# Layer 1 attention of a two-layer transformer: key and query transposes behind the scores of their slot, their evictions behind the block transpose and the block write

## The chip, the cores and the metric

The kernel runs on one NeuronCore of a Trainium2 chip, in one launch. The metric is the device time of the whole program in microseconds. A core has five engines that run their own instruction streams and meet only at semaphores: TensorE (PE in the profile; its weight loads are PEld), VectorE (DVE), ScalarE (ACT), GpSimd (POOL) and SyncE (SP), which here only issues DMA transfers. ScalarE issues one kind of transfer too; an engine that issues a transfer does so in its own program order. Each engine executes in order, so a wait holds everything behind it on that engine.

## The reference, cut to what matters

Two transformer layers on 1024 tokens of width 512, all in float32, with a layer norm after each part: a linear attention, a mixture of low-rank experts, a softmax attention and a quantised MLP. The change is in the softmax attention of layer 1:

```python
q = rmsnorm((hidden_states @ Wq + bq).reshape(b, n, H, HD), gq)     # H = 32, HD = 128
k = rmsnorm((hidden_states @ Wk + bk).reshape(b, n, H, HD), gk)
v = (hidden_states @ Wv + bv).reshape(b, n, H, HD)
scores = jnp.einsum('bhnd,bhmd->bhnm', q, k) * HD ** -0.5
out = jnp.einsum('bhnm,bmhd->bnhd', softmax(scores), v).reshape(b, n, H * HD)
return out @ Wo + bo
```

Scores are 1024 x 1024 for each head.

## The kernel before, in words

Float32 products are made of three matmuls (`three_pass`, L82 to L84): each operand is split into a high part, which ScalarE copies, and a low part, the rest, which VectorE or GpSimd subtracts. A value that comes from TensorE is therefore evicted from PSUM twice, high by ScalarE and then low by VectorE, which waits for the high part.

Layer 1's attention (`l1_attention`) is written out by hand as one stream for each engine. The outer loop goes over heads; one turn is called a step here, step h for head h. A step has eight slots, s = 0 to 7, one for each tile of 128 tokens. In slot s of step h these pieces of several heads stand side by side:

- TensorE: in even slots half of the value product of an earlier tile pair (`values`), then the projection of one tile of the next head to keys, queries and values (`project_tile`, 12 matmuls), in odd slots the transposes of a pair of tiles of keys and queries of head h + 1 (`transpose_kq`, four transposes, L1423), then `scores(h, b, s)` (six matmuls), `output_tile`, and in odd slots half of the value product.
- ScalarE, in this order: in even slots the squares for the norm; in odd slots the high part of values (`v_high`); in even slots the high part of an output pair; in odd slots the high parts of keys and queries (`kq_high`, L1325 and L1326); in even slots the high part of the transposed probabilities of a pair of tiles (`prob_hi`, L1354, two copies) and the scaling of keys and queries by their inverse norm (`scale_kq`, L1345); then `write_blocks(h, s - 1)`, a transfer issued from ScalarE (L1359); then `exponent(h, b, s)` (L1365); last, weight copies: for attention weights (`split_high`, L1039) in slots 1, 2 and 4, for the output weights in slot 3.
- VectorE: in even slots the mean squares (`means`); the projected tile plus bias (`take`, L1491); an output pair's low part or the inverse sums (in turn); in odd slots `kq_low` (L1507 and L1508); then `transpose_blocks(h, s - 1)` (L1521), then `maxima(h, b, s)` (L1515), the row maximum that `exponent` needs; then `add_output`.
- GpSimd: the inverse norms (`inverse_rms`), the low parts of values, of the probabilities (`prob_lo`, L1287) and of the weights.

The probabilities of a tile are transposed through memory: VectorE transposes within 32 x 32 blocks (L1521), ScalarE writes the tile to a buffer in HBM (512 KB, L1359), and SyncE reads it back block-wise with four transfers of 128 KB (`move`, L1242) into the place where `prob_hi` takes it. `move` waits for the landed write of its tile and, for each pair, for a free buffer. Tile 7 of head h is transposed, written and read back in slot 0 of step h + 1, and `prob_hi` takes tiles 6 and 7 in slot 2 of that step. SyncE's program for a step begins with the load of the attention weights of head h + 2 (768 KB, L1033) and of its bias (192 KB, L1227); they stand behind `move(h - 1, 6)` of the step before and ahead of `move(h - 1, 7)`:

```python
def step(h, b, cur, rest, nxt, more):
    if cur and more:
        aw.load(sp, w, h + 2)
        load_bias(h + 2, b)
    if rest:
        move(h - 1, NT - 1)
    for t in range(NT - 1):
        if cur:
            move(h, t)
```

`more` is false in steps 30 and 31, so these have no load and no weight copies. `cur` says that the head of this step has scores, `rest` that there is a head before, `nxt` that there is one after. Steps -2 to 1 and 30 to 32 are written out, the others are turns of a loop of two steps. The score sums have two buffers (`s_ps`), the tiles of keys and queries being transposed one (`kq_ps`), of which `transpose_kq` waits to be free by `kq_lo_done`.

Of the kernel before, what the change touches and what calls it, by code (L numbers as in the profile page):

```python
# [74 lines left out]
def f(ap):  # L75

    return ap.bitcast(F32)
# [972 lines left out]
def l1_attention(nc, sh, ln_in, ln, aw, mlp, w, ow, bias, bo, gains):  # L1050
# [16 lines left out]
    with ExitStack() as ctx:  # L1067
# [108 lines left out]
        def projected(h, b, nxt, more, s):  # L1176

            if s < 6:
                return (h + 1, 1 - b, s + 2) if nxt else None
            return (h + 2, b, s - 6) if more else None  # L1180
# [129 lines left out]
        @block.scalar  # L1310
        def _(act):
            for t in range(NT):
                ln_in.scalar_high(act, ln_banks, t)

            def square(g, i):
                act.wait_ge(taken, NT * g + BATCH * (i + 1))
                wait(act, summed, NB * g + i)
                act.activation(sq[:, :, :, :].rearrange("p t k d -> p t (k d)"), nat[i][:, :, 0:2 * HD],
                               ACT.Square).then_inc(squared, 1)

            def kq_high(g, bg, i):
                cut = slice(i * WIDE, (i + 1) * WIDE)
                act.wait_ge(kq_tr, NB * g + i + 1)
                wait(act, scored, NT * (g - 1))
                act.activation(k_hi[bg][:, cut], kq_ps[:, 0, :], ACT.Copy)  # L1325
                act.activation(q_hi[bg][:, cut], kq_ps[:, 1, :], ACT.Copy, scale=gain[:, 0:1]).then_inc(kq_hi_done, 1)  # L1326

            def v_high(g, bg, i):
                act.wait_ge(taken, NT * g + BATCH * (i + 1))
                wait(act, pv, NB * (g - 1))  # L1330
                act.activation(v_hi[bg][:, BATCH * i:BATCH * (i + 1), :], nat[i][:, :, 2 * HD:],
                               ACT.Copy).then_inc(v_hi_done, 1)

            def out_hi(h, i):
                act.wait_ge(pv, NB * h + i + 1)
                wait(act, y_done, NT * h + BATCH * (i - 1))
                act.activation(by_tile(o_hi[i % 2]), by_group(o_ps), ACT.Copy).then_inc(o_hi_done, 1)

            def scale_kq(g, bg, i):

                act.wait_ge(rstd_ready, NB * g + i + 1)
                for u in range(BATCH):
                    for k in range(2):
                        part = nat[i][:, u, k * HD:(k + 1) * HD]
                        last = act.activation(part, part, ACT.Copy, scale=rstd[bg][:, BATCH * i + u, k:k + 1])  # L1345
                last.then_inc(kq_scaled, 1)

            def prob_hi(h, i, part):

                act.wait_ge(moved[i % 2], MOVED * (2 * h + i // 2 + 1))  # L1350
                wait(act, pv, NB * h + i - 1)
                cut = slice(part * NT // 2, (part + 1) * NT // 2)
                raw, hi = (half[:, :, :, cut, :].rearrange("p g u m q -> p (g u) (m q)") for half in (pT_lo[i % 2], pT_hi[i % 2]))
                act.activation(hi, f(raw), ACT.Copy).then_inc(pT_hi_done, 1)  # L1354

            def write_blocks(h, t):

                act.wait_ge(blocked, NT * h + t + 1)
                act.dma_start(bounce[t % BOUNCES][:, :, :, :].rearrange("g p a n -> (g p) (a n)"),  # L1359
                              blocks[t % 2][:, :, :, :].rearrange("p a m q -> p (a m q)")).then_inc(written[t % 2], 16)  # L1360

            def exponent(h, b, t):
                act.wait_ge(shift_done, NT * h + t + 1)
                wait(act, blocked, NT * h + t - 1)
                act.activation(prob[t % 2][:, :], s_ps[t % 2][:, :], ACT.Exp, bias=shift[:, t:t + 1],  # L1365
                               accum_out=row_sum[:, t:t + 1]).then_inc(exp_done, 1)

            def step(h, b, cur, rest, nxt, more):
                if peeled(h, -1):
                    act.wait_ge(gain_ready, 1)  # L1370
                for s in range(NT):
                    if nxt and s % 2 == 0:
                        square(h + 1, s // 2)
                    if v_batch(h, b, cur, nxt, s):
                        v_high(*v_batch(h, b, cur, nxt, s))
                    q = quarter(h, b, cur, rest, s)
                    if q and q[3]:
                        out_hi(q[0], q[2])
                    if nxt and s % 2:
                        kq_high(h + 1, 1 - b, s // 2)  # L1380
                    if split_batch(h, cur, rest, s):
                        for part in range(2):
                            prob_hi(*split_batch(h, cur, rest, s), part)
                    if nxt and s % 2 == 0:
                        scale_kq(h + 1, 1 - b, s // 2)
                    if rest and s == 0:
                        write_blocks(h - 1, NT - 1)
                    if cur and s:
                        write_blocks(h, s - 1)
                    if cur:  # L1390
                        exponent(h, b, s)
                    if cur and s == 3:
                        act.wait_ge(ow_in, 16 * (h + 1))
                        wait(act, y_done, NT * (h - 1))
                        act.activation(ow_hi[b][:, :], ow_raw[:, :], ACT.Copy).then_inc(ow_hi_done, 1)
                    if nxt and more and s in SPLITS:
                        aw.split_high(act, h + 2, b, SPLITS[s])

            steps(act, step)

        @block.tensor
        def _(pe):
# [58 lines left out]
            def step(h, b, cur, rest, nxt, more):  # L1461
                for s in range(NT):
                    if s % 2 == 0 and quarter(h, b, cur, rest, s):
                        values(*quarter(h, b, cur, rest, s))
                    if projected(h, b, nxt, more, s):
                        project_tile(*projected(h, b, nxt, more, s))
                    if nxt and s % 2:
                        transpose_kq(h + 1, s // 2)
                    for t in scored_in(h, cur, s):
                        scores(h, b, t)  # L1470
                    if output(h, b, cur, rest, s):
                        output_tile(*output(h, b, cur, rest, s))
                    if s % 2 and quarter(h, b, cur, rest, s):
                        values(*quarter(h, b, cur, rest, s))
# [4 lines left out]
        def _(dve):  # L1479
# [65 lines left out]
            def step(h, b, cur, rest, nxt, more):  # L1545
                if peeled(h, -1):
                    dve.wait_ge(const_in, 32)
                    ln.link(dve, dve.tensor_tensor(gain[:, :], gain_in[:, 0:1], gain_in[:, 1:2], ALU.mult))
                    dve.tensor_scalar(gain[:, :], gain[:, :], float(HD) ** -0.5, None,
                                      ALU.mult).then_inc(gain_ready, 1)  # L1550
                    dve.wait_ge(gain_ready, 1)
                for s in range(NT):
                    q = quarter(h, b, cur, rest, s)
                    if nxt and s % 2 == 0:
                        means(h + 1, s // 2)
                    if projected(h, b, nxt, more, s):
                        take(*projected(h, b, nxt, more, s))
                    if peeled(h, -1):

                        dve.wait_ge(ln_in.tr, s + 1)  # L1560
                        dve.tensor_tensor(sh.x_nat[:, s, :], sh.x_nat[:, s, :], bo_sb[:, :], ALU.add).then_inc(
                            bias_added, 1)
                    if q and not q[3]:
                        invert_sums(q[0], q[2])
                    if q and q[3]:
                        out_lo(q[0], q[2])
                    if nxt and s % 2:
                        kq_low(h + 1, 1 - b, s // 2)

                    if rest and s == 0:  # L1570
                        transpose_blocks(h - 1, NT - 1)
                    if cur and s:
                        transpose_blocks(h, s - 1)
                    for t in scored_in(h, cur, s):
                        maxima(h, b, t)
                    if output(h, b, cur, rest, s):
                        add_output(*output(h, b, cur, rest, s))
# [350 lines left out]
```

## Time and profile before

| | |
|---|---|
| Median of 3 runs | 3117.12 us (3116.02 to 3117.77) |
| Profiled execution, its own time | 3121.27 us |
| Its span, first to last instruction | 3119.4 us |
| Mean granted clock of TensorE | 0.985 of full speed |
| TensorE busy | 2969.7 us, 95% of the span |
| VectorE busy | 1933.6 us, 62% |
| ScalarE busy | 1474.9 us, 47% |
| GpSimd busy | 1574.7 us, 50% |

Layer 1's attention reaches from about 1242 to 2856 us of the span, its scores from 1281.7 to 2820. A row of the timeline is one instruction, or several alike merged: its start and duration in us, engine, line, what it writes and reads, how many, and in brackets how long the engine sat idle before it and what ended that. Starts of TensorE's matmuls are closer together than their durations, since they are pipelined. ACTq and SPq are issues of transfers; their duration is that of the issue, not of the transfer.

### The profile page before, as it was taken

Reading aid. Unit: us, or ns where it says so; the run is one execution under the profiler, and the core shown is the slowest. Engines: PE = TensorE matmul, PEld = TensorE weight load, DVE = VectorE, ACT = ScalarE, POOL = GpSimd, SP = SyncE. Lnnn points to the kernel's source line nnn. Section 1 sums busy time; section 2 is a strip of 40 time slices with the busy share of each in tenths; the row PEclk is TensorE's granted clock in tenths of the full one; section 3 lists DMA queues with packets and bytes.
Section 4 is the critical chain, followed back from the end, with each engine's and each line's share of the span. In section 5 each row is a group of like instructions: output and inputs, shape, how many; then the busy total and the mean of one; then the engine's idle time right before and its main releaser. Section 6 shows DMA issues by size and latency. Waiting matters only on the chain. (4 is left out here: it accounts for less than half of the span.)

```text
span 3119.4 us, 56941 instructions
## 1 busy us (share of the span) xinstructions
PE 2969.7 (95%) x17632; PEld 2675.7 (86%) x17632; DVE 1933.6 (62%) x3061; ACT 1474.9 (47%) x2887; POOL 1574.7 (50%) x1075
## 2 busy tenths in 40 slices
PE   7999999999999978899999999999999999996998
PEld 7999999999999966799888898898988889885886
DVE  3445454545445455677777777777777777775565
ACT  3333333333333322566666666666666666653221
POOL 3333333333333331366666666666666666654764
PEclk9999999999999989999999999999999999998999
DMA  4112111122112101366665666666666566665551
GB/s 127 59 51 61 56 59 50 54 62 61 50 54 60 49 24 39 104 206 201 195 203 187 201 202 196 204 194 198 199 194 203 191 200 200 195 197 180 152 140 49
DMA packets 311499, 413.83 MB, mean 133 GB/s; under 512 B 35968, under 2 KB 242832, under 8 KB 311312
## 3 DMA queue, kind: packets, MB, share of 16 engines
q1 hardware_dynamic: 273728, 278.05, 31.7%
q10 hardware_dynamic: 37680, 135.02, 10.9%
q8 instruction: 32, 0.52, 0.1%
q14 instruction: 27, 0.22, 0.0%
q0 software_dynamic: 32, 0.02, 0.0%
HBM read 259.85 MB, written 136.31 MB: 127 GB/s over the span
## 5 line engine op out<-in xcount | busy, mean ns | idle before, releaser
L1365 ACT ACTIVATE b_prob<-b_s_ps,b_shift 128x1024 f32<-128x1024 f32 x256 | 285.4, 1115 | 479.1 <-DVE b_shift L1515 471.9
L82 PE MATMUL b_pj_kq<-b_w_hi,xT_hi 128*128 128x384 f32 x1008 | 344.5, 342 | 7.9 <-DVE b_nat L1491 6.6
L506 ACT ACTIVATE a_sig<-a_pj 128x512 f32<-128x512 f32 x192 | 114.9, 599 | 487.4 <-PE a_pj L84 487.3
L83 PE MATMUL b_pj_kq<-b_w_lo,xT_hi 128*128 128x384 f32 x1008 | 342.5, 340 | 0.0
L84 PE MATMUL b_pj_kq<-b_w_hi,xT_lo 128*128 128x384 f32 x1008 | 342.2, 340 | 0.0
L1287 POOL TENSOR_TENSOR b_pT_lo<-b_pT_lo,b_pT_hi 128x1024 fp32r<-128x1024 f32 x128 | 303.7, 2394 | 68.4 <-ACT b_pT_hi L1354 68.4
L1521 DVE STREAM_TRANSPOSE b_blocks<-b_prob 128x1024 f32<-128x1024 f32 x256 | 316.1, 1235 | 1.7 <-ACT b_prob L1365 1.7
L1287 POOL TENSOR_TENSOR pT_lo<-pT_lo,pT_hi 128x1024 fp32r<-128x1024 f32 x128 | 304.7, 2403 | 14.9 <-ACT pT_hi L1354 14.9
L82 PE MATMUL a_pj<-b_w_hi,xT_hi 128*128 128x256 f32 x1024 | 296.0, 289 | 11.3 <-DVE xT_lo L647 11.3
L1515 DVE TENSOR_REDUCE b_shift<-b_s_ps 128x1 f32<-128x1024 f32 x256 | 303.5, 1186 | 3.0 <-PE b_s_ps L84 3.0
L401 POOL TENSOR_TENSOR b_w_lo<-b_w_raw,b_w_hi 128x512 fp32r<-128x512 f32 x96 | 123.8, 1290 | 332.2 <-ACT b_w_hi L457 325.3
L84 PE MATMUL a_pj<-b_w_hi,xT_lo 128*128 128x256 f32 x1024 | 290.3, 283 | 0.0
L83 PE MATMUL a_pj<-b_w_lo,xT_hi 128*128 128x256 f32 x1024 | 289.9, 283 | 0.0
L1272 POOL TENSOR_TENSOR b_rstd<-b_mean_sq,power 128x4 f32<-128x4 f32 x128 | 128.9, 1007 | 305.0 <-DVE b_mean_sq L1501 298.4
L706 DVE TENSOR_TENSOR a_kv_nat<-a_pj,a_sig 128x512 f32<-128x512 f32 x128 | 88.6, 692 | 274.1 <-ACT a_sig L506 272.8
L711 DVE TENSOR_TENSOR a_acc<-a_acc,a_y_ps 128x512 f32<-128x512 f32 x252 | 170.6, 677 | 136.0 <-PE a_y_ps L84 136.0
L82 PE MATMUL b_s_ps<-b_k_hi,b_q_hi 128*128 128x512 f32 x512 | 213.4, 417 | 6.3 <-ACT b_prob L1365 6.3
L82 PEld LDWEIGHTS a_pj<-b_w_hi,xT_hi 128*128 128x128 f32 x1024 | 195.0, 190 | 14.1 <-issue 11.3
L82 PEld LDWEIGHTS b_pj_kq<-b_w_hi,xT_hi 128*128 128x128 f32 x1008 | 190.5, 189 | 19.4 <-POOL b_w_lo L1046 5.1
L84 PE MATMUL b_s_ps<-b_k_hi,b_q_lo 128*128 128x512 f32 x512 | 203.6, 398 | 0.0
L83 PE MATMUL b_s_ps<-b_k_lo,b_q_hi 128*128 128x512 f32 x512 | 203.2, 397 | 0.0
L83 PEld LDWEIGHTS a_pj<-b_w_lo,xT_hi 128*128 128x128 f32 x1024 | 195.4, 191 | 2.6
(257 smaller groups left out, 8830.7 us busy)
## 6 DMA issues: line engine op xcount, KB each, us to landing
bounce<-b_blocks ACTq DMA_DIRECT2D x256, 512.0 KB, 2.7
pT_lo<-bounce SPq DMA_DIRECT2D x512, 128.0 KB, 3.1
b_pT_lo<-bounce SPq DMA_DIRECT2D x512, 128.0 KB, 2.8
b_w_raw<-in_w SPq DMA_DIRECT2D x32, 768.0 KB, 5.7
b_w_raw<-in_w SPq DMA_DIRECT2D x95, 256.0 KB, 3.2
a_k_raw<-a_k_blocks SPq DMA_DIRECT2D x512, 32.0 KB, 1.8
a_w_raw<-in_w SPq DMA_DIRECT2D x32, 256.0 KB, 2.7
a_ow_raw<-in_ow SPq DMA_DIRECT2D x32, 256.0 KB, 3.1
```

The costliest lines, as they stand in the source:

```text
L82: pe.matmul(out, w_hi, x_hi, start=first, stop=False)
L83: pe.matmul(out, w_hi, x_lo, start=False, stop=False)
L84: return pe.matmul(out, w_lo, x_hi, start=False, stop=last)
L401: pool.tensor_tensor(w_lo[t][:, :, :], w_raw[t][:, :, :], f(w_hi[t][:, :, :]), ALU.subtract).then_inc(w_lo_done, 1)
L506: act.activation(out, pj[half][:, :], ACT.Sigmoid).then_inc(sig, 1)
L706: dve.tensor_tensor(out, pj[half][:, :], sig_tmp[half][:, :], ALU.mult).then_inc(silu, 1)
L711: dve.tensor_tensor(acc[:, t, :], acc[:, t, :], y_bank(h, t)[:, :], ALU.add).then_inc(y_added, 1)
L1272: pool.tensor_tensor(rstd[bg][:, BATCH * i:BATCH * (i + 1), :].rearrange("p t k -> p (t k)"), mean_sq[:, :, :].rearrange("p t k -> p (t k) ...
L1287: pool.tensor_tensor(lo, f(lo), f(hi), ALU.subtract).then_inc(pT_lo_done, 1)
L1365: act.activation(prob[t % 2][:, :], s_ps[t % 2][:, :], ACT.Exp, bias=shift[:, t:t + 1], accum_out=row_sum[:, t:t + 1]).then_inc(exp_done, 1)
L1515: dve.tensor_reduce(shift[:, t:t + 1], s_ps[t % 2][:, :], AX_X, ALU.max, negate=True).then_inc(shift_done, 1)
L1521: dve.transpose(blocks[t % 2][:, :, :, :].rearrange("p a m q -> p m a q"), prob[t % 2][:, :].rearrange("p (m a q) -> p m a q", a=GROUPS, q ...
```

## The change

In each odd slot the pieces that belong to the transposes of keys and queries move behind others of the same slot, on three engines:

```diff
 # ScalarE
-                    if nxt and s % 2:
-                        kq_high(h + 1, 1 - b, s // 2)
                     if split_batch(h, cur, rest, s):
...
                     if cur and s:
                         write_blocks(h, s - 1)
+                    if nxt and s % 2:
+                        kq_high(h + 1, 1 - b, s // 2)
                     if cur:
                         exponent(h, b, s)
 # TensorE
+                    for t in scored_in(h, cur, s):
+                        scores(h, b, t)
                     if nxt and s % 2:
                         transpose_kq(h + 1, s // 2)
-                    for t in scored_in(h, cur, s):
-                        scores(h, b, t)
                     if output(h, b, cur, rest, s):
                         output_tile(*output(h, b, cur, rest, s))
 # VectorE
-                    if nxt and s % 2:
-                        kq_low(h + 1, 1 - b, s // 2)
-
                     if rest and s == 0:
                         transpose_blocks(h - 1, NT - 1)
                     if cur and s:
                         transpose_blocks(h, s - 1)
+                    if nxt and s % 2:
+                        kq_low(h + 1, 1 - b, s // 2)
                     for t in scored_in(h, cur, s):
                         maxima(h, b, t)
```

Even slots keep their order, and no instruction or transfer is added or taken away.

## Rows read from the trace of the kernel before

**Rows 1.** Waits of steps 1 to 29: us in total, times, longest.
```profile
PE b_pj_kq L1423 <- ACT b_nat L1345: 41.2, 29, 2.1
ACT b_pT_hi L1354 <- DMA b_pT_lo<-bounce: 70.6, 29, 3.1
DVE b_nat L1491 <- PE b_pj_kq L84: 7.0, 19, 0.7
```

**Rows 2.** TensorE's timeline, slots 3 and 5 of step 15.
```profile
2026.53 0.66 PE L1423 MATMUL b_pj_kq<-ident,b_nat 128*128 128x128 f32 x4 [1.18 <-ACT b_nat L1345]
2026.94 0.48 PE L82 MATMUL b_s_ps<-b_k_hi,b_q_hi 128*128 128x512 f32 x1
...
2028.41 0.40 PE L82 MATMUL b_y_ps<-b_ow_hi,b_o_hi 128*128 128x512 f32 x1
...
2038.27 0.60 PE L1423 MATMUL b_pj_kq<-ident,b_nat 128*128 128x128 f32 x4
```

**Rows 3.** ScalarE's timeline: exponentials of step 1, step 15 and step 30.
```profile
1337.31 1.12 ACT L1365 ACTIVATE b_prob<-b_s_ps,b_shift 128x1024 f32<-128x1024 f32 x1 [3.14 <-DVE b_shift L1515]
...
2018.66 1.12 ACT L1365 ACTIVATE b_prob<-b_s_ps,b_shift 128x1024 f32<-128x1024 f32 x1 [3.14 <-DVE b_shift L1515]
...
2026.38 1.10 ACT L1365 ACTIVATE b_prob<-b_s_ps,b_shift 128x1024 f32<-128x1024 f32 x1
...
2038.55 1.11 ACT L1365 ACTIVATE b_prob<-b_s_ps,b_shift 128x1024 f32<-128x1024 f32 x1 [0.80 <-DVE b_shift L1515]
...
2044.37 1.12 ACT L1365 ACTIVATE b_prob<-b_s_ps,b_shift 128x1024 f32<-128x1024 f32 x1 [3.15 <-DVE b_shift L1515]
...
2050.34 1.12 ACT L1365 ACTIVATE b_prob<-b_s_ps,b_shift 128x1024 f32<-128x1024 f32 x1 [0.91 <-DVE b_shift L1515]
...
2055.63 1.12 ACT L1365 ACTIVATE b_prob<-b_s_ps,b_shift 128x1024 f32<-128x1024 f32 x1 [3.14 <-DVE b_shift L1515]
...
2061.65 1.12 ACT L1365 ACTIVATE b_prob<-b_s_ps,b_shift 128x1024 f32<-128x1024 f32 x1 [0.89 <-DVE b_shift L1515]
...
2748.73 1.12 ACT L1365 ACTIVATE b_prob<-b_s_ps,b_shift 128x1024 f32<-128x1024 f32 x1 [3.14 <-DVE b_shift L1515]
...
2754.70 1.12 ACT L1365 ACTIVATE b_prob<-b_s_ps,b_shift 128x1024 f32<-128x1024 f32 x1 [0.91 <-DVE b_shift L1515]
```

**Rows 4.** Timelines of SyncE and ScalarE, step 15; last, the page's transfers (KB, landing).
```profile
2011.37 0.36 SPq L1033 DMA_DIRECT2D b_w_raw<-in_w  x1
2012.18 0.33 ACTq L1359 DMA_DIRECT2D bounce<-b_blocks  x1
2018.57 1.90 SPq L1242 DMA_DIRECT2D b_pT_lo<-bounce  x4
2023.30 1.06 ACT L1354 ACTIVATE b_pT_hi<-b_pT_lo 128x1024 fp32r<-128x1024 f32 x1 [2.12 <-DMA b_pT_lo<-bounce]
...
bounce<-b_blocks ACTq DMA_DIRECT2D x256, 512.0 KB, 2.7
```

**Rows 5.** Timelines of ScalarE and VectorE, slot 7 of step 15.
```profile
2051.75 0.37 ACT L1325 ACTIVATE b_k_hi<-b_pj_kq 128x256 fp32r<-128x256 f32 x1
2052.52 0.42 DVE L1507 TENSOR_TENSOR b_k_lo<-b_pj_kq,b_k_hi 128x256 fp32r<-128x256 f32 x1 [1.03 <-ACT b_q_hi L1326]
2053.25 1.23 DVE L1521 STREAM_TRANSPOSE b_blocks<-b_prob 128x1024 f32<-128x1024 f32 x1
2054.41 1.19 DVE L1515 TENSOR_REDUCE b_shift<-b_s_ps 128x1 f32<-128x1024 f32 x1
```

**Rows 6.** Timelines of ScalarE and VectorE in the tail, step 31.
```profile
2797.84 1.10 ACT L1365 ACTIVATE b_prob<-b_s_ps,b_shift 128x1024 f32<-128x1024 f32 x1
2799.07 1.25 DVE L1521 STREAM_TRANSPOSE b_blocks<-b_prob 128x1024 f32<-128x1024 f32 x1 [0.18 <-ACT b_prob L1365]
2800.34 0.33 ACTq L1359 DMA_DIRECT2D bounce<-b_blocks  x1
2800.77 1.12 ACT L1365 ACTIVATE b_prob<-b_s_ps,b_shift 128x1024 f32<-128x1024 f32 x1 [1.43 <-DVE b_blocks L1521]
```

## The prediction, made before the changed kernel ran

> **What bounds the kernel now.** The change touches only the attention of layer 1, so I read that stretch, in this order. First the waits of steps 1 to 29. TensorE has one kind: the key and query transposes (L1423) wait for ScalarE's scaled keys and queries (L1345), 29 times, once per step, 41.2 us in all [rows 1]. Its own pace comes from its timeline: two sets of transposes with no stall between them start 11.74 us apart, so a step of four such pairs is 46.96 us of TensorE work [rows 2].
>
> Next the exponentials (L1365), one per slot, as a clock of the softmax side. From exponential 1 of step 1 to exponential 1 of step 30 lie 2748.73 - 1337.31 = 1411.42 us, 48.67 a step [rows 3]. TensorE needs 46.96, so 1.71 a step is lost. Is it lost in TensorE's stall, or in another chain that the stall merely shows? The rows speak for the second: before nearly every exponential ScalarE sat idle until VectorE's row maximum [rows 3], and VectorE waited for TensorE's projections only 7.0 us in 29 steps [rows 1]. ScalarE and VectorE run a chain of their own: exponential, key and query evictions, block transpose, maximum, next exponential. In one step its intervals are, slot 1 to 2: 7.72 (2026.38 - 2018.66), 2 to 4: 12.17, 4 to 5: 5.82, 5 to 6: 5.97, 6 to 7: 5.29, 7 to 0: 6.02 [rows 3]. Slots 0 to 1 do the work of 6 to 7, 5.29; 2 to 3 does that of 4 to 5, with a weight copy on ScalarE that costs 5.82 - 5.29 = 0.53; so 3 to 4 is 12.17 - 5.82 = 6.35. The sum is 48.28, this step's period.
>
> The long one, 1 to 2, holds ScalarE's wait for a transfer: the high part of the probabilities (L1354) waits for the last blocks of the head before, 29 times, 70.6 us, 2.43 a step [rows 1], 2.12 in the step shown [rows 4]. ScalarE's path there is 2023.30 - 2.12 - 2018.66 = 2.52 before that wait and 2026.38 - 2023.30 = 3.08 behind it: 5.60 plus the wait. The path over VectorE I take from step 30, whose slot 2 has no wait: 2754.70 - 2748.73 = 5.97 [rows 3], plus the weight copy that step 30 lacks, 0.53, is 6.50. So of the mean 2.43, 0.90 is free and 1.53 is paid. Without that wait the chain would take 47.1 a step: two limits 0.2 apart, TensorE's and the chain's.
>
> Why is the transfer late? Block write 7 is issued at 2012.18 and its first read back at 2018.57: 6.39 us, where the median write lands in 2.7. Beside it runs the 768 KB weight load, which SyncE issued 0.81 before, at 2011.37 [rows 4]. In SyncE's program the load comes right behind the reads of tile 6, and those wait for write 6.
>
> **The change part by part.** Nothing is added or removed; three moves in each odd slot.
>
> TensorE: four transposes go behind the six score matmuls. The work is the same. The wait they meet (mean 41.2 / 29 = 1.42, longest 2.1 [rows 1]) now comes after the scores, 2028.41 - 2026.94 = 1.47 from their start to that of the output tile [rows 2], and behind it stand the output tile and half of the values, no longer the scores. For this stall alone the cover is about complete.
>
> ScalarE and VectorE: the odd interval from one exponential to the next. Before: exponential, key copy 1.41 later (2051.75 - 2050.34), VectorE's low parts 0.77 later, block transpose 0.73, maximum 1.16, exponential 1.22 (2055.63 - 2054.41): 5.29 [rows 3, 5]. After: the block transpose needs only the exponential. From the exponential to the block transpose is 1.23 and from there to the issue of the write 1.27, read in the tail, where VectorE stood idle waiting for the exponential [rows 6]. The key copy is now queued behind the issue; the tail shows ScalarE's next instruction 0.43 behind one (2800.77 - 2800.34) [rows 6]. Then 0.77, 0.73 and 1.22 as before: 1.23 + 1.27 + 0.43 + 0.77 + 0.73 + 1.22 = 5.65. Value copy and weight copy now lie beside the block transpose, in which ScalarE waits anyway, so all four odd slots cost 5.65: 22.60 against 5.29 + 5.82 + 5.82 + 5.29 = 22.22. The change makes this part 0.38 a step longer. The uncertain piece is what an issue costs the instruction behind it: nothing if the two ran side by side, and at most the 1.11 by which exponential 7 trails its issue (2055.63 - 2053.25 - 1.27), though that is the maximum's time; at 1.11 a step would be 50.2. I take 0.43, the only row where the next instruction comes right behind.
>
> The key copy also needs the transposes, now later on TensorE: scores 1.47, then the transposes 0.41 (2026.94 - 2026.53), some 2.1 behind the start of the scores with the way to ScalarE. The scores start within 0.6 us of the exponential before (2026.94 against 2026.38) [rows 2, 3], the key copy comes 1.23 + 1.27 + 0.43 = 2.93 behind it. Cost nothing; if TensorE fell over 0.2 further back, the interval would grow one for one, but TensorE would then be the late one and nothing on it would wait for this.
>
> Transfers: the writes of tiles 0, 2, 4 and 6 are issued 2.50 behind the exponential instead of 1.41 + 0.77 + 0.73 + 1.27 = 4.18, so 1.68 earlier. SyncE's queue follows: reads of tile 6, weight load, bias load. Write 7 (an even slot, order unchanged) comes 5.65 - 5.29 = 0.36 later. So the load leads write 7 by 0.81 + 1.68 + 0.36 = 2.85 instead of 0.81. From load to landed write took 7.20 (2018.57 - 2011.37). If the same bytes take the same time, write 7 lands 4.35 behind its issue, 2.04 sooner; if the load is wholly out of its way, 2.7 behind, 3.7 sooner; if contention keeps it as it is, 0. I take 2.04, the one that the rows carry. The reader in slot 2 comes 0.36 later by the longer interval 0 to 1. New wait: 2.43 - 2.04 - 0.36 = 0.03, in the worst step (3.1 [rows 1]) 0.7. Up to 0.90 is free, so the paid 1.53 is gone.
>
> Sum of a step: 22.60 + 6.50 + 6.35 + 5.97 + 6.02 = 47.44 against 48.67: 1.23 less, over 29 steps 35.7. Step 30 has no weight copies to hide and no wait in slot 2: its four odd slots give back 1.4; step 0 perhaps 0.5. Net 33.8. The profiled execution took 3121.3 us, so 3087.5; it lay 4.2 above the median of the runs, 3117.1, and in those terms the forecast is 3083.
>
> The Trainium skill (Perfetto Trace Analysis, Identifying the Most-Contended Engine) says to find the engine with the highest occupancy and optimize that one first. By that rule closing TensorE's gaps is the whole prize, the first rival below, about 3069; the exponentials' rows show a second chain just behind, so the rule would promise some 14 us too much here.
>
> **Rivals.**
> TensorE takes over: the chain comes out at or under 46.96, as it would if the key copy ran beside the issue (odd slots 5.65 - 0.43 = 5.22, a step 45.7). Then 1.71 x 29 = 49.6 is saved, less what the edges give back: 3069. For it: the stall is real. Against it: the 0.43 row.
> Part of the wait stays: write 7 lands only about 1 us sooner and the chain still pays 0.2 to 0.9 a step: 3089 to 3109.
> Hidden anyway: the landing does not move. The wait shrinks only by the 0.36 of its later reader, slots 0 to 2 together stay as they are, the other three odd slots change by +0.36 - 0.17 - 0.17: 48.7 a step, and TensorE's stall only changes place. 3117 to 3120. For it: the 41.2 us on TensorE are no bound of their own.
> Slower: the earlier writes fall into the reads of the odd tiles. Today tile 5's write is issued in slot 6, 1.16 + 1.22 - 1.27 = 1.11 before exponential 6; it lands 2.7 later, the four reads take 1.90 to issue and the last lands 2.83 on (2023.30 - 2018.57 - 1.90) [rows 4]: 6.3 behind exponential 6. Its copy in slot 0 comes 5.29 + 2.52 - 0.53 = 7.3 behind it: slack 1.0, with the longer interval 1.3. Tile 3 for slot 6 has 1.3 too (6.3 against 5.82 + 1.99, less 0.17). Write 6 would now be issued 2.50 behind exponential 6, in the flight of those reads, and write 4 likewise. If each is stretched as write 7 is today, 6.39 - 2.7 = 3.7, slots 0 and 6 pay 3.7 - 1.3 - 0.9 = 1.5 each: 3.0 - 1.23 = 1.8 x 29, with the edges 3170. It decides from a stretch of 2.8 on. Against it: 512 KB meet 512 KB there, where write 7 meets 960 KB and reads as well. The Trainium skill (DMA: Bandwidth & Descriptors, Issuing engines are not separate DMA queues) has transfers from ScalarE and SyncE interleave on the same engines, which is what makes the collision possible; the 6.39 agrees.
>
> **How the numbers follow.** Forecast 0.50 (own range 3078 to 3090), TensorE takes over 0.14, part of the wait 0.16, hidden 0.09, slower 0.11. The range holds the first three: 3064 to 3112. A difference under 0.2% (6 us) cannot be told from none. Faster 0.80, same 0.09, slower 0.11.
>
> **What would show it.** Right: L1354's wait for a transfer falls below 0.9 a step; the odd exponential intervals are all near 5.65; write 7 to its first read near 4.4; the load 1.7 earlier against exponential 6; a step 47.4. Wrong: odd intervals near 5.2 or over 6; write 7 still over 6 us; L1354 waiting in slots 0 or 6; value matmuls waiting for the low parts where the transposes waited.

## The result, and the profile after

The changed kernel takes 3101.23 us in the median (3099.54 to 3102.95, 5 runs) against 3117.12 (3114.54 to 3117.77, 5 runs): ratio 0.9948, 95% interval 0.9937 to 0.9959, 15.9 us faster. I had forecast 33.8. The sign is right and the time lies between the outer bounds that I gave, 3064 and 3112, but outside the forecast's own range, 3078 to 3090: 15.9 of the 33.8 us came.

First the waits of ScalarE and TensorE over the steps 1 to 29 of the kernel after; the same view as [rows 1].

```profile
ACT b_prob L1365 <- DVE b_shift L1515: 319.6, 224, 2.0
ACT b_k_hi L1325 <- DVE b_blocks L1521: 148.5, 117, 1.5
ACT b_pT_hi L1354 <- DMA b_pT_lo<-bounce: 11.3, 23, 1.1
...
PE b_pj_kq L82 <- DVE b_nat L1491: 12.4, 54, 0.5
```

The 70.6 us that ScalarE waited for the last blocks are 11.3. TensorE's stall of 41.2 at the transposes is gone too; what it waits for instead, 12.4 us, is VectorE taking the projected tile out of the bank. A new wait of 148.5 us stands on ScalarE: the key copy for the block transpose, the queue order that the change made.

Now the clock of the softmax side, as in [rows 3]: four of ScalarE's exponentials of the kernel after, 6 and 7 of step 15 and 0 and 1 of step 16.

```profile
2040.36 1.12 ACT L1365 ACTIVATE b_prob<-b_s_ps,b_shift 128x1024 f32<-128x1024 f32 x1 [0.92 <-DVE b_shift L1515]
2046.16 1.12 ACT L1365 ACTIVATE b_prob<-b_s_ps,b_shift 128x1024 f32<-128x1024 f32 x1 [2.01 <-DVE b_shift L1515]
2052.18 1.12 ACT L1365 ACTIVATE b_prob<-b_s_ps,b_shift 128x1024 f32<-128x1024 f32 x1 [0.88 <-DVE b_shift L1515]
2057.99 1.12 ACT L1365 ACTIVATE b_prob<-b_s_ps,b_shift 128x1024 f32<-128x1024 f32 x1 [2.02 <-DVE b_shift L1515]
```

The odd intervals, 2046.16 - 2040.36 and 2057.99 - 2052.18, are 5.80 and 5.81, the even one 6.02 as before. In nearly all steps the odd intervals are 5.80 or 5.81, and the interval 1 to 2 is 6.38 or 6.44 where it was 7.4 to 8.7. Over the 29 steps the four odd intervals make 23.21 in place of 22.19, the four even ones 24.77 in place of 26.48. From the first exponential of step 1 (1333.09) to that of step 30 (2724.30) the 29 steps take 47.97 us each in place of 48.67.

Inside an odd interval, VectorE and ScalarE of the kernel after, slot 7 of step 15; the rows that answer to [rows 5] and [rows 6].

```profile
2041.69 1.25 DVE L1521 STREAM_TRANSPOSE b_blocks<-b_prob 128x1024 f32<-128x1024 f32 x1 [0.18 <-ACT b_prob L1365]
2042.97 0.33 ACTq L1359 DMA_DIRECT2D bounce<-b_blocks  x1
2043.40 0.38 ACT L1325 ACTIVATE b_k_hi<-b_pj_kq 128x256 fp32r<-128x256 f32 x1 [1.53 <-DVE b_blocks L1521]
2044.18 0.42 DVE L1507 TENSOR_TENSOR b_k_lo<-b_pj_kq,b_k_hi 128x256 fp32r<-128x256 f32 x1 [1.25 <-ACT b_q_hi L1326]
2044.92 1.22 DVE L1515 TENSOR_REDUCE b_shift<-b_s_ps 128x1 f32<-128x1024 f32 x1
```

Exponential to block transpose 1.33, to the issue 1.28, to the key copy 0.43, to the low parts 0.78, to the maximum 0.74, to the exponential 1.24. ScalarE sits idle in the first half and VectorE in the second: the two engines take turns.

Last SyncE's and ScalarE's issues around write 7 of the kernel after, as in [rows 4].

```profile
2046.96 1.73 SPq L1242 DMA_DIRECT2D b_pT_lo<-bounce  x4
2049.20 0.36 SPq L1033 DMA_DIRECT2D b_w_raw<-in_w  x1
2050.99 0.33 ACTq L1359 DMA_DIRECT2D bounce<-b_blocks  x1
2055.94 1.77 SPq L1242 DMA_DIRECT2D b_pT_lo<-bounce  x4
```

The load now leads write 7 by 1.79 instead of 0.81, and the first read of what it wrote is issued 4.95 us after the write instead of 6.39; over the loop's steps the means are 4.92 and 6.33.

### The profile page after: what moved, and what is told of

The parts are those of the page before. It is cut to its first block and busy times, and to the rows that moved or that the text cites. A ratio compares the mean times of both kernels' runs of the same rounds, so it can differ in the third digit from the quotient of the medians.

```text
span 3097.8 us, 56941 instructions
## 1 busy us (share of the span) xinstructions
PE 2976.4 (96%) x17632; PEld 2666.8 (86%) x17632; DVE 1946.6 (63%) x3061; ACT 1490.4 (48%) x2887; POOL 1574.9 (51%) x1075
## 5 line engine op out<-in xcount | busy, mean ns | idle before, releaser
L82 PE MATMUL b_pj_kq<-b_w_hi,xT_hi 128*128 128x384 f32 x1008 | 351.7, 349 | 21.6 <-DVE b_nat L1491 20.1
L82 PE MATMUL a_pj<-b_w_hi,xT_hi 128*128 128x256 f32 x1024 | 295.6, 289 | 11.9 <-DVE xT_lo L647 11.3
L401 POOL TENSOR_TENSOR b_w_lo<-b_w_raw,b_w_hi 128x512 fp32r<-128x512 f32 x96 | 123.7, 1289 | 332.3 <-ACT b_w_hi L457 325.4
L82 PE MATMUL b_s_ps<-b_k_hi,b_q_hi 128*128 128x512 f32 x512 | 201.9, 394 | 6.5 <-ACT b_prob L1365 6.5
L1046 POOL TENSOR_TENSOR b_w_lo<-b_w_raw,b_w_hi 128x512 fp32r<-128x512 f32 x96 | 124.0, 1293 | 151.3 <-ACT b_w_hi L1039 133.6
```

Of the source, the lines that this page charges most:

```text
L82: pe.matmul(out, w_hi, x_hi, start=first, stop=False)
L401: pool.tensor_tensor(w_lo[t][:, :, :], w_raw[t][:, :, :], f(w_hi[t][:, :, :]), ALU.subtract).then_inc(w_lo_done, 1)
L1046: pool.tensor_tensor(self.lo[b][:, :, cut], self.raw[:, :, cut], f(self.hi[b][:, :, cut]), ALU.subtract).then_inc(self.lo_done, 1)
```

## The experiments

Theory A: ScalarE and VectorE's chain sets the step, and the gain is the shorter wait for the last blocks. Theory B: the gain is TensorE's, whose stall now stands behind the scores. "Before" in the ratios is the kernel before, run beside each of them. "Step" is the mean of steps 1 to 29 in each trace. ScalarE's part alone can't run: its key copy would wait for the block transpose, which on VectorE would stand behind the low parts, and these wait for the key copy.

| kernel | median us | ratio to before, 95% interval | step us |
|---|---|---|---|
| whole change | 3101.2 | 0.9948 (0.9937 to 0.9959) | 47.97 |
| TensorE's part alone | 3134.4 | 1.0056 (1.0043 to 1.0070) | 49.24 |
| VectorE's and ScalarE's parts | 3101.1 | 0.9954 (0.9940 to 0.9967) | 48.00 |
| VectorE's part alone | 3066.4 | 0.9843 (0.9829 to 0.9856) | 46.98 |
| VectorE's and TensorE's parts | 3068.2 | 0.9854 (0.9841 to 0.9868) | 46.96 |
| before, load late | 3181.2 | 1.0218 (1.0200 to 1.0236) | 50.94 |
| whole, load late | 3235.4 | 1.0386 (1.0369 to 1.0402) | 52.76 |
| before, load and copies late | 3086.6 | 0.9907 (0.9892 to 0.9922) | 47.60 |
| whole, load and copies late | 3116.5 | 1.0003 (0.9994 to 1.0012) | 48.56 |
| VectorE's part, load and copies late | 3063.4 | 0.9834 (0.9820 to 0.9847) | 46.91 |
| whole, write issued behind the copies | 3099.7 | 0.9937 (0.9924 to 0.9950) | 46.3 and 49 to 51 in turn |

**TensorE's part alone.** The diff is the TensorE part of the change.

> One part alone: only TensorE's transposes of keys and queries go behind the scores; ScalarE and VectorE keep the order of before. Theory A (the chain of ScalarE and VectorE sets the step, and the change gained by taking the wait for the last blocks out of slot 2): that wait stays at some 2.4 us a step, the step stays near 48.6 us, TensorE's stall moves elsewhere: 3114 to 3122 us, no gain. Theory B (the gain came from TensorE's stall, which now stands behind the scores): the step falls towards 46.96, at least the 16 us that the whole change gave: 3076 to 3101 us.

Measured: 17 us slower than before. Its waits in steps 1 to 29:

```profile
ACT b_pT_hi L1354 <- DMA b_pT_lo<-bounce: 68.6, 29, 2.9
...
PE b_pj_kq L82 <- DVE b_nat L1491: 24.3, 29, 0.9
PE b_pj_kq L1423 <- ACT b_nat L1345: 15.5, 27, 1.0
ACT b_k_hi L1325 <- PE b_pj_kq L1423: 14.1, 50, 0.5
```

TensorE's stall fell from 41.2 to 15.5 and the kernel got slower. Theory B is out. The wait for the last blocks stayed (68.6), and the key copy, still at its early place, now waits for the transposes: the odd intervals 6 to 7 and 0 to 1 grew from 5.30 to 5.57 and 5.77 in the mean, those with a weight copy stayed. Theory A foretold the missing gain but not this loss.

**VectorE's and ScalarE's parts**, TensorE as before.

> The other two parts: evictions of keys and queries behind block transpose and block write on VectorE and ScalarE, transposes ahead of the scores as before. Theory A: odd intervals 5.81, slot 2's wait for a transfer under 0.9, step 48.0: 3099 to 3104 us, the time of the whole change. Theory B: TensorE still meets its stall ahead of the scores, so 3115 us or more.

Measured: the time, the step and the odd intervals (5.80, 5.81) of the whole change. TensorE's part is worth nothing in it: its stall at the transposes is 2.9 us in 29 steps here though its order is untouched.

**VectorE's part alone.**

```diff
                     if q and q[3]:
                         out_lo(q[0], q[2])
-                    if nxt and s % 2:
-                        kq_low(h + 1, 1 - b, s // 2)
...
                     if cur and s:
                         transpose_blocks(h, s - 1)
+                    if nxt and s % 2:
+                        kq_low(h + 1, 1 - b, s // 2)
```

> VectorE's part alone: kq_low behind the block transpose; ScalarE copies keys and queries ahead of the block write as before, so the copies lie beside the block transpose. Theory A: odd interval = exponential to block transpose 1.33, to the low parts 1.16, 0.74, 1.24 = 4.5 (4.7 with a weight copy), writes of even tiles as early as in the whole change, chain some 44 us a step, so TensorE's 46.96 sets it: 3117 - 1.6 x 29 = 3070 us. Theory B: nothing is changed on TensorE, its stall stays: 3112 to 3120 us.

Measured: 3066.4, 51 us under before and 35 under the whole change. Slot 3 of step 15, on ScalarE and VectorE, from exponential 2 to exponential 3:

```profile
1997.58 1.12 ACT L1365 ACTIVATE b_prob<-b_s_ps,b_shift 128x1024 f32<-128x1024 f32 x1 [0.21 <-DVE b_shift L1515]
1999.14 1.23 DVE L1521 STREAM_TRANSPOSE b_blocks<-b_prob 128x1024 f32<-128x1024 f32 x1
1999.52 0.37 ACT L1325 ACTIVATE b_k_hi<-b_pj_kq 128x256 fp32r<-128x256 f32 x1
2000.29 0.42 DVE L1507 TENSOR_TENSOR b_k_lo<-b_pj_kq,b_k_hi 128x256 fp32r<-128x256 f32 x1
2002.27 1.12 ACT L1365 ACTIVATE b_prob<-b_s_ps,b_shift 128x1024 f32<-128x1024 f32 x1 [2.02 <-DVE b_shift L1515]
```

The key copy runs while VectorE transposes the blocks. The odd interval is 4.69 here, where a weight copy stands ahead of the key copy, and 4.5 in the mean where none does. With that the chain has room and the step is TensorE's. The waits of steps 1 to 29:

```profile
DVE b_nat L1491 <- PE b_pj_kq L84: 147.0, 230, 1.4
...
ACT b_pT_hi L1354 <- DMA b_pT_lo<-bounce: 51.5, 36, 2.9
...
PE b_pj_kq L1423 <- ACT b_nat L1345: 1.4, 4, 0.6
```

TensorE's stall at the transposes is 1.4 us in all, and VectorE now waits 147.0 us for TensorE's projections, where it waited 7.0. A wait for the last blocks is still there (51.5) and costs little or nothing: where it is 18.3, with load and copies late, the time is only 3 us lower.

**VectorE's and TensorE's parts.** Against the whole change only ScalarE's order differs.

> VectorE's and TensorE's parts, ScalarE as before: differs from the whole change only in that the copies of keys and queries are issued ahead of the block write. Theory A: the copies wait for the transposes, not for the block transpose and the issue of the write, TensorE sets the step at 46.96: 3068 to 3075 us. Theory B: same as the whole change, 3101 us, since TensorE's order is the same.

Measured: 3068.2, within 2 us of VectorE's part alone, with the step at TensorE's 46.96. So the 33 us between this kernel and the whole change are ScalarE's part of it, the eviction behind the block write.

**The load late.**

```diff
-                if cur and more:
-                    aw.load(sp, w, h + 2)
-                    load_bias(h + 2, b)
                 if rest:
                     move(h - 1, NT - 1)
+                if cur and more:
+                    aw.load(sp, w, h + 2)
+                    load_bias(h + 2, b)
```

> The kernel before with one edit on SyncE: the load of the attention weights and bias is issued behind the reads of tile 7 instead of ahead of them; all orders on TensorE, ScalarE and VectorE are those of before. If the load is what makes write 7 land 6.4 us late: it lands in about 2.7, slot 2's wait for a transfer falls below 0.9, odd intervals stay 5.29 and 5.82, step 47.1: 3117 - 1.4 x 29 = 3073 to 3080 us. If the load isn't the cause: wait and step stay, 3115 to 3119 us.

> The whole change with the same SyncE edit (weight load behind the reads of tile 7). Theory A says that the changed kernel pays nothing for the transfer any more and that its odd intervals of 5.81 set the step: 48.0 stays, 3099 to 3103 us, though the late load is gone. If a part of the transfer's wait is still paid in the changed kernel: the step falls by that part, down to 47 and 3075 us.

Both times missed by a long way, because the edit brought a wait that I had not counted. ScalarE's waits for transfers in the kernel before with the late load, steps 1 to 29:

```profile
ACT b_w_hi L1039 <- DMA b_w_raw<-in_w: 98.2, 29, 5.1
...
ACT b_pT_hi L1354 <- DMA b_pT_lo<-bounce: 2.9, 1, 2.9
```

The wait for the last blocks is gone (70.6 to 2.9) and write 7 is read back 2.63 us after its issue, so the load is what made it late. The load did not lose its neighbour, it changed it: write 0 of the head that follows, which the load now meets, takes 7.2 us to its first read instead of 3.4, and almost nothing waits for that one. But the weights themselves now come too late for their first copy in slot 1 (3.4 us each time), and TensorE waits behind it, 71.9 us here and 106.9 in the whole change. The pair says nothing clean on the step, hence the next.

**Load and copies late.** As above, with one line more; on the kernel before, the whole change, and VectorE's part.

```diff
-        SPLITS = {1: 0, 2: 1, 4: 2}
+        SPLITS = {2: 0, 3: 1, 4: 2}
```

> The kernel before with the weight load behind the reads of tile 7, and the three weight copies (high and low) one slot later where the load would not have landed: in slots 2, 3 and 4 instead of 1, 2 and 4. So neither the collision nor a wait for the weights is left. If the late landing of write 7 is what cost 1.5 us a step: odd intervals 5.29 to 5.82, step 47.1, 3117 - 1.5 x 29 = 3070 to 3080 us. If the chain pays something else instead: step over 48 and 3100 us or more.

> The whole change with the same two edits (weight load behind the reads of tile 7, weight copies in slots 2, 3 and 4). Theory A: the changed kernel pays nothing for the transfer; its four odd intervals of 5.81 and even ones of 24.8 set the step at 48.0, so 3099 to 3103 us again. If part of the transfer's wait were still paid: below 3095 us.

> VectorE's part alone with the same two edits. Its step stood at 47.0 with TensorE free of stalls, so theory A (TensorE's 46.96 is the floor there, not the transfer) has it unchanged: 3064 to 3068 us. If the wait for the transfer (50.6 us in all in that kernel) were paid: 3040 to 3055 us.

ScalarE's waits for the last blocks, first in the kernel before, then in the whole change, with both edits:

```profile
ACT b_pT_hi L1354 <- DMA b_pT_lo<-bounce: 1.3, 1, 1.3
```

```profile
ACT b_pT_hi L1354 <- DMA b_pT_lo<-bounce: 0.6, 1, 0.6
```

The kernel before gains 29 us and has a step of 47.60, not the 47.1 expected; the whole change loses 15 and misses its forecast too. Both for one reason: a copy moved from slot 1 to slot 3 takes 0.5 from the interval 1 to 2 (5.86 or 5.92) and adds 1.1 to 3 to 4 (7.5), 0.6 a step. With that taken off, the whole change stands at 48.56 - 0.6, its own 47.97: it pays nothing for the transfer, which is what the run was to tell. The kernel before, so corrected, stands at 47.0 against 48.67: the late landing cost it 1.7 a step, of which 1.6 in the interval 1 to 2. The correction is taken from the whole change and is not itself a run. VectorE's part alone moves by 3 us and the intervals of its two ratios overlap: it is at TensorE's floor.

**The issue behind the copies.** On the whole change:

```diff
                     if cur and s:
-                        write_blocks(h, s - 1)
+                        act.wait_ge(blocked, NT * h + s)
                     if nxt and s % 2:
                         kq_high(h + 1, 1 - b, s // 2)
+                    if cur and s:
+                        write_blocks(h, s - 1)
```

> The whole change with one edit in the odd slots of ScalarE: the copies of keys and queries still wait for the block transpose, but stand ahead of the issue of the block write instead of behind it. It measures the price of the issue by itself. In the trace of the changed kernel the copy starts 0.43 us behind the issue, so the odd interval should fall from 5.81 to 5.38 and the chain to 46.3 a step, under TensorE's 46.96: the step is then TensorE's, 3101 - 1.0 x 29 = 3072 us (3068 to 3080), though the writes of even tiles go out some 0.7 us later. If the issue costs the chain nothing and only the wait for the block transpose does: step 48.0, 3098 to 3103 us.

Measured: the odd interval is 5.38, as forecast, against 5.80 or 5.81, so the issue costs the chain 0.43, but the time hardly moved. One step in two takes 46.3, the other 49 to 51. The pauses behind the slow ones lie in slot 0, at the start of a turn of the loop, where ScalarE stops twice with nothing to wait for; first its timeline, then the instruction queue in the page of that kernel, last the same queue between 1946 and 1960 us:

```profile
1949.99 0.63 ACT L1318 ACTIVATE b_sq<-b_nat 128x512 f32<-128x512 f32 x1 [1.92 <-issue]
...
1952.75 2.01 ACT L1354 ACTIVATE pT_hi<-pT_lo 128x1024 fp32r<-128x1024 f32 x2 [1.85 <-issue]
```

```profile
q14 instruction: 92, 0.75, 0.1%
...
q14 instruction: 4, 0.03, 0.7%
```

In the whole change that queue has 27 packets, and none in that window. The 65 more are five in each of 13 turns of the loop, and these 13 are the turns with the pauses: all but the first, so those that a jump back leads to. In the turn shown three of the five start at 1947.35, 1947.87 and 1951.04, about the two pauses of 1948.07 to 1949.99 and 1950.90 to 1952.75. The edit makes ScalarE's turn longer, from 262 recorded instructions to 268, and from then on part of it seems to be fetched anew in each turn. That the fetch is the pause is read from the packets' count and times; no run varied the length of the loop alone.

**Before again**, for a second profile.

> The kernel before, unchanged, for a second profile: the first profiled execution lay 4 us above the median of its runs. If that is a matter of how long the wait in slot 2 happens to be, the step here is near 48.5 instead of 48.67 and the time near 3117 us; odd intervals are 5.29 and 5.82 again.

Measured: 3119.99 us, step 48.69. The guess was wrong: this profiled execution too lies above the median of the runs beside it, by 4.6, with a step like the first's.

## Why the prediction was wrong

*What bounds the kernel.* Right. TensorE's stall only showed the chain: taking 26 us of it away alone cost 17. The wait for the last blocks was worth 1.53 in my sum and 1.6 to 1.7 by the runs, and the weight load was its cause.

*TensorE's move.* I gave it no value, which is right in the whole change. "Cost nothing" for the key copy's wait on the transposes holds only because ScalarE's move puts the copy later; alone it cost.

*ScalarE and VectorE, the term that failed.* The mechanism was right, the size of one term was not: I had each odd interval at 5.65 and it is 5.80. Four a step over 29 steps are 17.6 us, and the even intervals, 24.77 against my 24.84, give 2 back: of the 35.7 us of gain in these steps some 20 were left. Two thirds of the miss are one part, exponential to block transpose, 1.23 in my rows from the tail [rows 6] and 1.33 in the loop; the rest is 0.01 or 0.02 in each of four other parts. The issue, which I called the uncertain piece, was right at 0.43.

The 0.10 goes with the loop. Step 1 of the kernel after is written out, like step 31 of my rows; from its exponential 6 to its exponential 7:

```profile
1368.64 1.12 ACT L1365 ACTIVATE b_prob<-b_s_ps,b_shift 128x1024 f32<-128x1024 f32 x1 [0.79 <-DVE b_shift L1515]
1369.87 1.25 DVE L1521 STREAM_TRANSPOSE b_blocks<-b_prob 128x1024 f32<-128x1024 f32 x1
1374.35 1.12 ACT L1365 ACTIVATE b_prob<-b_s_ps,b_shift 128x1024 f32<-128x1024 f32 x1 [2.02 <-DVE b_shift L1515]
```

To the block transpose it is 1.23 there, and the odd interval is 5.71; step 30, written out too, has the same. In the 28 steps of the loop it is 1.33 in nearly all odd slots. There the trace has an operation of 45 ns on VectorE's sequencer that waits for the exponential and starts 1.24 behind its start, and the block transpose starts 0.09 behind that; in steps 1 and 30 there is no such operation and the transpose itself has the wait. That the wait's count, which in the loop depends on the loop's variable, is the reason fits this but is argued: no run took the loop away. In the kernel before, VectorE never had to wait for an exponential in these steps, so no row of the loop could have shown me this part. I took sureness from having a row for each part; but where the gain is the small difference of two sums of 47, 0.15 in each odd slot is half of it.

*Transfers.* The direction was right, the size not. The load leads write 7 by 1.8 and not 2.85, since write 6, issued 2.6 behind exponential 6, takes 4.0 to its first read (2046.96 - 2042.97) where it took 2.9 in the mean. It now goes out 1.08 behind the first read of tile 5 (2041.89) where it was 2.66, and writes 2 and 4, moved alike, take 3.8 to 4.0 instead of 2.65, while writes 1, 3 and 5 stay at 2.63: the mechanism of my slower rival at a third of its price. The mean wait is 11.3 / 29 = 0.39, not 0.03. Nothing was paid for the miss, because 0.90 was free: the interval 1 to 2 keeps its 6.38 or 6.44 in 26 of the 29 steps, whatever the wait.

*The edges.* I had them give back 1.9. The exponentials place step 1's start 1.1 later (1333.09 against 1332.02) and the stretch behind step 30's start 2.5 shorter (3097.8 - 2724.30 against 3119.4 - 2743.43): 1.4 gained, by luck, since no term of mine has it. With the 0.70 x 29 = 20.3 of the steps that is 21.7, just what the profiled executions differ by (3121.27 - 3099.54). The medians differ by 15.9. The other 6 are that the profile of before lies 4.2 above its median and that of after 1.7 below; the second profile of before lies 4.6 above, too, and why is open. So of the 17.9 us between the forecast gain and the measured one, the odd intervals account for 17.6; the even ones and the edges gave back 5.5, and this offset took 5.8.

*The rivals.* "TensorE takes over" is what happens as soon as ScalarE keeps its order. "Part of the wait stays" had a time near the measured one, for a reason that the load-and-copies run excludes.

## What to carry to other kernels

When the busiest engine has one regular stall, take the period between two like instructions on the other engines as well: here a chain of two engines that wait for each other had nearly the same period, and filling the stall alone made the kernel 17 us slower. When reordering such a chain, move work on the engine where it then lies beside the partner's, and leave it ahead of any wait on that partner: the same eviction was worth 51 us moved on VectorE alone and 16 when ScalarE moved with it. And where a gain is the difference of two nearly equal sums, take each part from the steady loop, or, where only code outside the loop has a row for it, widen the forecast to the size of that error.

## What was not expected of the hardware

A few more waits in ScalarE's instruction stream (268 instructions in a turn of the loop instead of 262, 57045 in all instead of 56941) raised the packets of an instruction queue from 27 to 92 and brought two pauses of about 1.9 us in 13 of the loop's 14 turns. VectorE's block transpose, waiting for an exponential, started 1.33 us behind its start in the loop and 1.23 in the same code written out. A weight load of 768 KB, with 192 KB behind it, issued 0.8 us ahead of a 512 KB write took the write from 2.7 to 6.4 us; at 1.8 us ahead it was 5.0.
